# A decoder block with sixteen routed experts: expert loads in four parts, scores applied where the outputs are evicted, and outputs summed by accumulating gathers

## The reference

```python
scores = softmax(xt @ Wg.T)                     # (T, 16)
# of 4 groups of 4 experts the 2 with the highest maximum stay, of those the top 4 experts
combine[t, topi] = scores[t, topi]
h = silu(einsum('td,eid->eti', xt, W1)) * einsum('td,eid->eti', xt, W3)   # I = 352
y = einsum('etd,te->td', einsum('eti,edi->etd', h, W2), combine)
z = silu(xt @ Ws1.T) * (xt @ Ws3.T) @ Ws2.T      # shared, 704 wide
x = x + y + z                                    # xt is the layer norm of x
```

## Time and profile before

| | us |
|---|---|
| median of 3 runs | 1986.05 (1982.33 to 1999.04) |
| the profiled execution | 1992.53 |
| its span, first to last instruction | 1990.8 |
| PE, DVE, ACT, POOL busy | 1538.8, 1064.9, 625.9, 659.5 |
| mean granted TensorE clock | 0.883 of full speed |

### The profile page before, as it was taken

One profiled execution on the slowest core, in us unless ns is written; L12 is line 12 of the kernel. 1 busy time (PEld: TensorE's weight loads), 2 busy tenths in 40 slices (PEclk: granted clock), 3 DMA queues, 4 the chain that ended last, 5 costly groups with the idle time before them and its releaser, 6 DMA issues. The chain is left out here.

```text
span 1990.8 us, 28736 instructions
## 1 busy us (share of the span) xinstructions
PE 1538.8 (77%) x9512; PEld 712.8 (36%) x9521; DVE 1064.9 (53%) x1809; ACT 625.9 (31%) x1103; POOL 659.5 (33%) x617
## 2 busy tenths in 40 slices
PE   2778787875287888887888488076889898989987
PEld 1344444432022222222222153033555455556543
DVE  6343434346387888888885586021333333334376
ACT  4322121212135666666666452010111111111121
POOL 3000000002463333333310226712645363653274
PEclk9989898988558999999999769587999899999998
DMA  4252516160453121222110102516545545553365
GB/s 169 73 171 57 186 44 198 32 211 29 117 170 78 38 65 36 43 51 54 28 28 1 46 1 92 204 69 244 160 123 154 130 126 163 152 130 89 114 190 172
DMA packets 177498, 211.05 MB, mean 106 GB/s; under 512 B 89296, under 2 KB 134928, under 8 KB 175120
## 3 DMA queue, kind: packets, MB, share of 16 engines
q1 hardware_dynamic: 153936, 119.27, 22.9%
q0 software_dynamic: 12832, 71.44, 10.2%
q10 hardware_dynamic: 10656, 19.40, 2.6%
HBM read 101.09 MB, written 88.87 MB: 95 GB/s over the span
## 5 line engine op out<-in xcount | busy, mean ns | idle before, releaser
L804 DVE TENSOR_REDUCE ca_mx<-ca_sc 128x1 f32<-128x512 f32 x512 | 328.0, 678 | 86.1 <-PE ca_sc L724 85.8
L77 PE MATMUL re_ab<-re_w,re_xt 128*128 x1800 | 316.4, 329 | 67.9 <-DMA re_xt<-slot_rows 57.1
L937 ACT ACTIVATE ca_pt<-ca_st 128x512 f32<-128x512 f32 x512 | 264.8, 596 | 99.9 <-PE ca_st L736 99.9
L77 PEld LDWEIGHTS re_ab<-re_w,re_xt 128*128 128x128 f16 x1800 | 180.6, 102 | 178.7 <-issue 74.5
L724 PE MATMUL ca_sc<-ca_ks,ca_qs 48*128 48x512 f16 x512 | 189.1, 424 | 51.5 <-DVE ca_mx L804 30.3
L736 PE MATMUL ca_st<-ca_qs,ca_ks 49*128 49x512 f16 x512 | 170.9, 397 | 41.0 <-ACT ca_pt L937 35.4
L77 PE MATMUL re_yp<-re_w,re_ht 128*128 (+1 forms) x666 | 156.0, 379 | 0.0
L1485 POOL TENSOR_TENSOR re_w<-re_raw_w,re_w 128x272 f16<-128x272 f32 x224 | 155.6, 731 | 1.1
L749 PE MATMUL ca_pv<-ca_pt,ca_va 128*32 128x512 f32 x1024 | 149.3, 647 | 1.0 <-DVE ca_turned L817 0.5
L478 POOL TENSOR_TENSOR sa_yt<-sa_yf,sa_yt 128x512 f16<-128x512 f32 x16 | 18.5, 1157 | 386.2 <-ACT sa_yt L461 386.2
L1590 DVE COPY re_ht<-re_ht_ps 128x768 f16<-128x768 f16 x74 | 41.3, 558 | 179.3 <-PE re_ht_ps L1513 179.3
(11 more groups left out here) (237 smaller groups left out, 2423.7 us busy)
## 6 DMA issues: line engine op xcount, KB each, us to landing
re_raw_w<-in_we POOLq DMA_DIRECT2D x14, 2176.0 KB, 10.0
slot_rows<-sa_zeros SPq DMA_DIRECT2D x12, 1792.0 KB, 15.9
slot_outs<-re_ys ACTq DMA_DIRECT2D x74, 256.0 KB, 2.0
sa_scratch<-sa_qk SPq DMA_DIRECT2D x16, 512.0 KB, 4.6
ca_scratch<-ca_qk SPq DMA_DIRECT2D x64, 128.0 KB, 1.8
sa_qs<-sa_scratch SPq DMA_DIRECT2D x12, 512.0 KB, 6.7
sa_ks<-sa_scratch SPq DMA_DIRECT2D x12, 512.0 KB, 6.9
ca_qs<-ca_scratch SPq DMA_DIRECT2D x48, 128.0 KB, 3.7
```

Of the source, the lines that this page charges most:

```text
L77: last = nc.tensor.matmul(out, lhs(a, c), rhs(b, c), start=(c == 0 and n == 0), stop=(c == chunks - 1 and n == len(PRODUCTS) - 1))
L804: nc.vector.reduce_max(mx[:, qd // 4, qd % 4, 2 * a + jj:2 * a + jj + 1], sc[:, m % RING, :], AX.X).then_inc(maxed, 1)
L937: nc.scalar.activation(pt[:, (4 * qd + k) % 8, :], st[:, m % RING, :], ACT.Exp, scale=SCALE).then_inc(exp_done, 1)
```

## The change

1. `slot_rows` becomes float32 rows of `ROW = D + E` = 528 words (2112 bytes): the 2048 bytes of the pair and behind them the row's 16 scores, which DVE copies into `rows` before `routed`. The twelve operations that made `route["weight"]` go.
2. In `routed_experts` SyncE, after each `turn_rows`, also loads the scores of tile t (one word of each of the 128 rows, in the column of the expert that owns the tile) into `slot_weight[:, s]`, and reads the owners from a register once in a turn. DVE's eviction (L1594) becomes a multiply by that scalar and waits for its load.
3. The pairs of experts 0 and 1 are loaded by SyncE at the start of the block in `route_and_share`; `w` moves out of `routed_experts` for that.
4. POOL loads expert 2 in four parts after the first tile's `ab_done`, waits for them, loads expert 3, waits, loads the shared weights, waits, and splits these in 8 pieces each. In the loop each quarter of the raw buffer is loaded anew as soon as its four subtracts are done.
5. In `combine_and_share` the gathers write `total`, 16 tiles: the first of each tile copies, the other three add in the DMA (`compute_op=ALU.add`), each after the one before it on the same tile. DVE does only the shared expert's work in the loop; behind it 16 adds of `total` to `x_sb` follow.
6. Smaller: the zeros that clear `slot_rows` are 528 words wide, and SyncE clears the first layer norm's semaphores.

```diff
+            for dram, pair, loaded in first_pairs:
+                sp.dma_start(pair, dram).then_inc(loaded, 16)
...
             step(nc.vector.tensor_scalar(route["index"][:, :, :], top[:, :, 0:TOPK], -1.0, None, ALU.add))
-            nc.vector.memset(hit[:, :, :], 0.0).then_inc(routed, 1)
+            nc.vector.tensor_copy(rows[:, :, D:ROW], s[:, :, :]).then_inc(routed, 1)
             for t in range(4):
                 shared.add(dve, x_sb, t)
-            dve.wait_ge(routed, 1)
-            for k in range(TOPK):
-                tk = top[:, :, k:k + 1].to_broadcast([P, NT, E])
-                step(nc.vector.tensor_tensor(hit[:, :, :], slot1[:, :, :], tk, ALU.is_equal))
-                step(nc.vector.tensor_tensor(hit[:, :, :], hit[:, :, :], s[:, :, :], ALU.mult))
-                step(nc.vector.reduce_sum(route["weight"][:, :, k], hit[:, :, :], AX.X))
...
+            def load_weights(s, tile, owner):
+                sp.dma_start(slot_weight[:, s:s + 1],
+                             tiles[bass.ds(tile, 1), :, bass.ds(owner + D, 1)].rearrange("o p n -> (o p) n"),
+                             allow_slow_non_contiguous=True).then_inc(weight_loaded[s], 16)
...
             with sp.Fori(0, n) as i:
+                owners = sp.value_load(route["owners"][0:1, bass.ds(2 * i, 1)], min_val=0, max_val=OWNER ** 3 - 1)
                 for s in range(2):
 
                     sp.wait_ge(ab_done, 2 * i + s + 1)
                     sp.sem_inc(slot_free, 1)
                     turn_rows(s, 2 * i + 2 + s)
+                    sp.wait_ge(ys_ready, 2 * i + s + 1)
+                    sp.sem_inc(slot_free, 1)
+                    load_weights(s, 2 * i + s, (owners >> (4 * s)) & (OWNER - 1))
...
-            for e in range(2):
-                pool.dma_start(w[:, e, :, :], we_pairs[e]).then_inc(pairs_loaded[e], 16)
-            for dram, raw, _pair in jobs:
-                pool.dma_start(raw, dram).then_inc(jobs_loaded, 16)
-            load_raw(2)
-            load_raw(3)
+            def load_raw(e, share):
+                at = slice(share * (WC // LOADS), (share + 1) * (WC // LOADS))
+                pool.dma_start(raw_w[:, e % 2, at], we_dram[e, :, at]).then_inc(raw_loaded[e % 2], 16)
+
             for e in range(2):
                 pool.wait_ge(pairs_loaded[e], 16)
                 pool.sem_inc(w_ready, 1)
+            pool.wait_ge(ab_done, 1)
+            for share in range(LOADS):
+                load_raw(2, share)
+            pool.wait_ge(raw_loaded[0], 16 * LOADS)
+            for share in range(LOADS):
+                load_raw(3, share)
+            pool.wait_ge(raw_loaded[1], 16 * LOADS)
+            for dram, raw, _pair in jobs:
+                pool.dma_start(raw, dram).then_inc(jobs_loaded, 16)
             pool.wait_ge(jobs_loaded, 16 * len(jobs))
             for n, (_dram, raw, pair) in enumerate(jobs):
-                nc.gpsimd.tensor_copy(pair[0], raw).then_inc(jobs_done, 1)
-                pool.wait_ge(jobs_done, n + 1)
-                nc.gpsimd.tensor_tensor(pair[1], raw, pair[0], ALU.subtract)
+                width = raw.shape[-1]
+                for at in range(0, width, width // (SHARES // 2)):
+                    part = slice(at, at + width // (SHARES // 2))
+                    nc.gpsimd.tensor_copy(pair[0][:, part], raw[:, part]).then_inc(jobs_done, 1)
+                    pool.wait_ge(jobs_done, n * SHARES // 2 + at // (width // (SHARES // 2)) + 1)
+                    nc.gpsimd.tensor_tensor(pair[1][:, part], raw[:, part], pair[0][:, part], ALU.subtract)
...
-                last.then_inc(w_ready, 1)
-                if e + 2 < E:
-                    pool.wait_ge(w_ready, e + 1)
-                    load_raw(e + 2)
+                for share in range(SHARES):
+                    at = slice(share * (WC // SHARES), (share + 1) * (WC // SHARES))
+                    nc.gpsimd.tensor_tensor(w[:, e % 2, 1, at], raw_w[:, e % 2, at], w[:, e % 2, 0, at], ALU.subtract
+                                            ).then_inc(w_low, 1)
+                    if e + 2 < E and share % (SHARES // LOADS) == SHARES // LOADS - 1:
+                        pool.wait_ge(w_low, SHARES * (e - 2) + share + 1)
+                        load_raw(e + 2, share // (SHARES // LOADS))
+                pool.wait_ge(w_low, SHARES * (e - 1))
+                pool.sem_inc(w_ready, 1)
...
                     dve.wait_ge(y_stored[s], 16 * i + 16)
-                    nc.vector.tensor_copy(ys[:, s, :], yp[:, s, :]).then_inc(ys_ready, 1)
+                    dve.wait_ge(weight_loaded[s], 16 * i + 16)
+                    nc.vector.tensor_scalar(ys[:, s, :], yp[:, s, :], slot_weight[:, s:s + 1], None, ALU.mult
+                                            ).then_inc(ys_ready, 1)
...
+            for k in range(TOPK):
+                for t in range(NT):
+                    if k:
+                        pool.wait_ge(summed[t], 16 * k)
+                    nc.gpsimd.indirect_dma_start(
+                        out=total[:, t, :], out_offset=None, in_=slot_outs,
+                        in_offset=bass.IndirectOffsetOnAxis(ap=route["index"][:, t, k:k + 1], axis=0),
+                        compute_op=ALU.add if k else ALU.bypass).then_inc(summed[t], 16)
...
             for g in range(shared.ROUNDS + 1):
-
                 for n in range(g * IC, min(g * IC + IC, shared.HIDDEN)):
                     shared.product(dve, nc.vector, n)
-                    combine(2)
                     shared.low_part(dve, nc.vector, n)
-                    combine(2)
                 if g >= 1:
                     for t in range(4 * g - 4, 4 * g):
-                        dve.wait_ge(used, len(fetches) - len(order))
                         shared.add(dve, x_sb, t)
-                        dve.wait_ge(shared.added, shared.tiles + t + 1)
-                        combine(1)
-            combine(len(order))
+            for t in range(NT):
+                dve.wait_ge(summed[t], 16 * TOPK)
+                dve.wait_ge(shared.added, shared.tiles + t + 1)
+                nc.vector.tensor_tensor(x_sb[:, t, :], total[:, t, :], x_sb[:, t, :], ALU.add).then_inc(used, 1)
```

80 lines of the change are left out of this document (33 added, 47 removed).

## The result

The changed kernel takes 1969.6 us (median of 13 runs, 1957.9 to 1977.9), the kernel before beside it 1987.0 (13 runs, 1977.3 to 2004.0). The ratio is 0.9898, 95% interval 0.9867 to 0.9930: faster by 1.0%, where 1938 us and 2.4% were forecast. The time lies inside the range, near its upper end. Over all of these the medians are 1965.8 us (31 executions) and 1992.5 us (67), a gain of 27 us or 1.3%. The forecast gain was 48 us. Two of those 67 executions ran over 1.5% above the fastest beside them and are left out of the ratios.

The account below looks back on a forecast made before the run. The routed stage was taken as PE's own, stalled by late turned rows. From 1992.5 us, -64.4 + 9 + 3.7 + 2 + 1.2 = -48.5 gave 1944.0, less 6.5 from profile to median: 1938 us, range 1908 to 1978.

Parts of the forecast that it names:

- loop from expert 2 on (-64.4 + 9 + 2): Routed loop: stalls gone -64.4 us, late POOL splits +9, slow clock after PE's long stand +2.
- combining: Last stage: PE's waits for DVE go, but 16 adds stand behind its last matmul; +1.2 us.
- The stalls (-64.4): Routed stage: 12 stalls of PE for turned rows `re_xt`, caught under whole loads, all vanish with loads in four; -64.4 us.
- POOL late (+9): Routed loop: POOL's longer splits make experts 3, 11, 12 and 13 about 1 us late, with slow clock; +9 us.
- DVE is busy 178 of 497 us: Routed stage: DVE's busy time, cited where the eviction's multiply by a scalar was put at nothing.
- Expert 2 (+3.7): Start of routed stage: POOL's loads and splits make PE stand some 26 us, until 1416.6 us; +3.7 us.
- The zeros, the wide rows and the early pairs (nothing): Ahead of routed stage: zeros grow 3% beside attention, wider rows leave scatter issue unchanged, early pairs load under low DMA share; no cost.
- rival 1: Combining: accumulating gathers at 1.9 to 2.85 us each set the end, giving 1970 us; chance 0.13.
- Profile to median (-6.5): Whole kernel: the median shown, 1986.05 us, lies 6.5 us below the profile, taken off the sum.
- Rivals 2: Combining: accumulating gathers go one at a time, 4.1 us each, giving 2046 us, slower; chance 0.10.
- 3: Routed loop: loads in parts act as before, the 64.4 us of stalls stay, giving 1993 us; chance 0.08.
- Rival 4: POOL is not late: loads 8.3 us, pieces 12.3, PE on at 1404, four-tile experts find weights; 1916 us; chance 0.07.

Follow-up runs that it names:

- first pair: First profiles of both kernels: the kernel before at 1992.5 us and the changed kernel at 1957.9 us.
- run 9: The kernel before, unchanged, for a second profile: median 1992.3 us, profiled execution 1982.7 us.
- run 10: The changed kernel as it is, on the chip of run 9: 1965.6 us, ratio 0.9869 to the kernel before.
- run 2: The changed kernel with each loop expert loaded in one DMA after its split, as before: 2010.6 us, ratio 1.0089.
- run 11: The changed kernel with shared expert's load and split behind splits of experts 4 to 9, CASTs in four, plain gathers with VectorE additions: 1927.1 us, ratio 0.9676.
- run 3: The changed kernel with POOL's CAST of each expert cut into eight pieces: 1968.3 us, ratio 0.9871.
- run 16: The changed kernel with POOL waiting for each of an expert's 16 subtracts before the next, CASTs whole: 1973.3 us, ratio 0.9902.
- run 4: The changed kernel with the shared expert's load behind expert 3's split and its split behind those of experts 4 to 7: 1950.1 us, ratio 0.9804.
- run 14: The joined version with the old 2048 B rows, weights, unscaled eviction and multiply-adds of the kernel before: 1886.3 us, ratio 0.9641.
- run 5: The changed kernel with plain gathers into a ring of 8, summed by VectorE without a scale: 1923.7 us, ratio 0.9848, on another kind of chip.
- run 6: The kernel before with only the loads of experts 4 to 15 cut in four parts: 1912.1 us, ratio 0.9785.
- joined version: The changed kernel with late shared-expert load and split, CASTs in four, plain gathers with additions; measured twice: 1927.1 us (0.9676) and 1892.2 us (0.9665).

## Why the prediction was wrong

By its own terms, from profile to profile: forecast -48.5 us, found -34.6 in the first pair and -17.0 in the second (runs 9 and 10). The medians, -27, lie between, since the first pair has a short execution of the changed kernel and the second a short one of before.

| step | forecast | first pair | second pair |
|---|---|---|---|
| loop from expert 2 on (-64.4 + 9 + 2) | -53.4 | -49.6 | -42.1 |
| up to expert 2's first matmul | +3.7 | +7.1 | +13.8 |
| combining | +1.2 | +7.8 | +11.2 |

The stalls went as forecast. Three steps failed. The largest is combining, sized at +1.2 and measured at +7.8 and +11.2. The second is what stands ahead of the scatter, put at nothing and measured at +4.9, which is part of the table's second row. The third is VectorE in the loop, taken as having room, where the long `re_hp` cost 13.2 us; this one nearly cancels in the sum, by luck, as the second point below says.

- **The stalls (-64.4)** were right in mechanism, and the size was right for the profile that it was read from. The waits are gone, and run 2 brings them back, 45 us above the changed kernel. From expert 2 on, -64.4, the 13.2 us of the next point and 1.7 us of a slow first tile after the stand make -49.5, found -49.6. In the second profile of before the stalls are 57 us. In run 11's loop PE is busy 442 of 452 us, so little more is to be had there. The Trainium skill's cost of one DMA ("DMA: Bandwidth & Descriptors", Anatomy of one DMA — SWDGE (gpsimd) path) gives 3.3 us a part, and as an estimate from it, with the parts one after another, 13 us for four; expert 2's four were issued from 1353.76 and all had landed by 1363.84, 10.1 us with the issues in it. The trace disagrees with that sum. (The section Measured, which the prediction names for the cost too, has only the rule of 1 MiB.)
- **POOL late (+9)** named the wrong loser, and its nearness to what was found is luck. POOL's split was sized well (1402.17 to 1420.02, 17.9 us for 18.5). But the subtracts, now in rows of four with an issue between, collide with `re_hp`. A tile so hit takes 7.06 us (1439.30 to 1446.36) instead of 5.86, 1.2 us in each of eleven experts, 13.2 us. That delay gave POOL the time it lacked. Where the collision goes (runs 3, 11 and 16), the late experts of the forecast appear, 3, 11, 12 and 13, and PE waits for them 6.6, 6.2 (with a first wait at expert 2) and 9.1 us. So the two are alternatives. The step that failed is "DVE is busy 178 of 497 us", a busy share read as room: it says nothing of what VectorE's single operation costs when POOL's instructions lie beside it.
- **Expert 2 (+3.7)**: the chain on POOL was 29.1 + 19.3 + 17.9 us, forecast 31 + 19 + 18.5. Its start was 5.7 us late (1353.8 instead of 1348.1), because the stage starts later. Run 4 takes the stand away and gains 15.6 us, and no other late work appears. That 50 us of loads and of another split stand ahead of it was in the prediction; that it is the largest single thing to mend was not said.
- **The zeros, the wide rows and the early pairs (nothing)**: the first scatter is 4.9 us later. PE waits 7.0 us more for `sa_ks`, so the cover, "beside the attention", was a DMA that PE waits for; of this 2.5 us are left where cross-attention begins (512.3 instead of 509.8). From cross-attention's last matmul to the shared expert's first the time grew from 49.3 to 52.1 us, and no run separates the causes of that; run 14, which has the early pairs but not the wide rows, has 51.2. Run 14 gains 5.9 us in the median by taking rows and weights back. In the second pair the scatter starts 11.1 us later, and 5.6 of that lie between cross-attention's first and last matmul, where nothing was changed.
- **Combining (+1.2)**: the time r of an accumulating gather was taken as 1.3 to 1.8 us and is 1.85, just where POOL's issue becomes the longer side; rival 1's bound began at 1.9. The last data landed some 8 us after POOL was done with their issue, not 3.4. With both, the prediction's own sum gives 30 + 48 x 1.85 + 5 = 124, found 125.1 us, so the model held and its inputs did not. With plain gathers the stage is 113.1 us beside 124.8 on one chip (runs 11 and 10) and 110.3 on another (run 5), so the part given up is 12 to 15 us.
- **Profile to median (-6.5)**: the 1992.5 us of before is also the pooled median, so nothing was to be taken off. The 1957.9 of after is 8 us below its own. Its profile had 42 us from the last scatter to the routed loop, the lower of the two levels (42 and 53 to 56; before 47 and 48). That goes some way to explain why the medians gain 27 and the first profiles 35. What chooses the level was not found. From cross-attention's first matmul to the shared expert's, too, the changed kernel took 667 us in two profiles and 670 and 674 in two others, with a granted clock of 0.86 and 0.85; the reason stays open.

Rivals 2 and 3 are out (gathers 1.85 apart, stalls gone). Rival 4 is out by its own terms: the three loads took 29.1 us, not 25, the pieces 19.3, not 12.3, and PE went on at 1420, not 1404. Only its second half came true, that experts of four tiles find their weights, and for another reason than it gives.

## What to carry to other kernels

Loads cut in four, with their parts spaced by other work, no longer stall the small transfers beside them that PE waits for, and this although the DMA share of the routed stage rose from 0.46 to 0.56. Alone they are worth 2.2% (run 6), and with everything else in the change 1.3% were left (on other chips). Before work is queued ahead of a split that PE waits for, ask whether it is needed by then: moved behind, it was free. An accumulating gather that saves time on an idle VectorE costs POOL 0.6 us each, and POOL's issue was what ended the kernel. The joined version with plain gathers and the old weights (run 14) is at 0.9641 (0.9614 to 0.9669), 3.6% faster than before. Take a second profile of the kernel before: here it moved the loop by 8 us and the last stage by 4.

## What the hardware did that was not expected

- A VectorE subtraction with both inputs in SBUF (0.53 us alone) took up to 3.5 us beside POOL's subtracts, by where in their row it began: 3.5 where a row of four began 0.45 us after it, 2.1 where it began 1.0 us inside one (run 3), but 0.7 at nearly the same place in the changed kernel, 1.06 at most in the rows of 16 of before, and 0.98 at most with a pause between any two. `re_hf`, `re_ht` and `re_ys`, which read PSUM, kept 0.53, 0.56 and 0.75 us beside the same subtracts. The Trainium skill ("SBUF — State Buffer", Who interferes with whom) says that a VectorE instruction with two inputs in SBUF contends with a GpSimd instruction that reads it, and one with at most one such input outside the two-port modes does not. By that rule the trace agrees: only `re_hp` grows. The runs add that such a subtraction can be held over up to four of POOL's instructions in a row, to the end of the row, and at other places gets through between two of them.
- While 64 scatters are issued, signals between PE and VectorE come late on some chips (PE waits 32 to 58 us in all for `x_sb`, single waits of 20 to 40) and not on others (7.4 us in every profile): before took 1987 to 1996 us on the one kind and 1952 to 1959 on the other. The joined version was run on both, with ratios of 0.9676 and 0.9665; the changed kernel only on the first kind.
